# Filtered read pass of a four-layer GNN kernel: who builds the second half of the gather's one-hot columns

## The chip, the cores and the metric

One core of one Trainium2 chip. The metric is the device time of one execution of the whole program in microseconds, and the kernel before is given by the median of three executions.

## What is computed

The program runs four graph layers over 12,500 nodes and 400,000 edges (edges sorted by `dst`), with a residual and a layer norm after each:

```python
x = layernorm(x + L0(x, W, edge_weight, src, dst))          # weighted sum over edges, relu
x = layernorm(x + L1(x, src, dst, edge_attr_64, ...))       # filtered messages, below
x = layernorm(x + L2(x, edge_index, W1, b1, W2, b2))        # sum over edges, then an MLP
x = layernorm(x + L3(x, edge_index, weight, bias))          # degree-normalised sum

def L1(x, i, j, rbf, ...):                                  # i = src, j = dst
    Wxh  = x @ Wl.T + bl
    f_ij = silu(rbf @ Wf1.T + bf1) @ Wf2.T + bf2
    agg  = segment_sum(f_ij * Wxh[j], i, num_segments=12500)
    ...
```

The change touches layer L1 alone: the gather `Wxh[j]`, the product with the filter rows `f_ij` and the sum into row `i`.

## The kernel before, in words

Edges were sorted by an earlier stage (`fused`) into cells of up to 128 edges: the node rows of `dst` are cut into NW = 49 windows of 256 nodes, those of `src` into NS = 98 tiles of 128 nodes. `read_pass(1, filtered=True)` (L1326) does layer L1. It walks over GW = 14 groups of CG = 7 source tiles, and in each group over the 49 windows. One window of one group is a step: 686 steps, each over seven cells of 128 edges. Seven steps are a round (RUN = 7, seven rounds to a group). Of the seven rounds the first six are a hardware loop, with addresses and semaphore targets made from registers; the last is written out, its table offset a constant.

A step j does the following.

- **first** (VectorE, L1401 to L1409): `row` holds, on all 128 partitions, the position (1 to 256) of each of the 896 edges in its window. Two tensor_scalar instructions at L1407 compare it with partition + 1 (m = 0) and partition + 129 (m = 1, `iota2`), giving the two halves of `hot`, [128, 2, 7, 128] in bf16. Position 0 marks an empty place.
- **gather** (TensorE, L1487 to L1500): 42 matmuls (seven cells, two halves, three bf16 parts of the table) of 64 columns each gather the table's rows into PSUM. It waits for `x_hot` of its step and for `x_whole` two steps back.
- **message** (VectorE, L1418 to L1438) in three pieces: `whole` = gathered rows times filter rows (L1427), `rest` = whole minus its bf16 head (L1433), and the third part (L1437), which signals `x_msg`.
- **second** (VectorE, L1411, by way of `selection` at L552): the one-hot columns for the sum.
- **scatter** (TensorE, L1510 to L1519): seven matmuls of 193 columns into four PSUM banks. It waits for `x_sel` and `x_msg`.
- **taken** (ScalarE, L1563 to L1569): once in a group, four copies of the sums out of PSUM. `collect` (VectorE, L1440) adds the parts. After `taken`, TensorE clears the banks (L1523).

The order on each queue is written out by hand. VectorE in step j: whole(j), first(j + 2), rest(j), second(j + 1), third part(j). TensorE: gather(j + 1), scatter(j), gather(j + 2), scatter(j + 1), and so on; so gather(j + 1) is behind scatter(j - 1), which waits for third part(j - 1). `hot`, `sel` and `msg` have three buffers each, used in the order 0, 1, 0, 1, 0, 1, 2. SyncE reloads `row`, `pairs` and `f` in spans of two steps, the row after `x_hot` of the span, the pairs after `x_sel`, the filter rows after `x_whole` (L1374). ScalarE has nothing but `taken` in this pass.

`reach` (L1306) is a wait for a semaphore against a value made from the step's number, and `settle` (L132, recorded at L135) is an instruction that carries such waits.

Of the kernel before, what the change touches and what calls it, by code (L numbers as in the profile page):

```python
# [8 lines left out]
ACT = mybir.ActivationFunctionType  # L9
# [29 lines left out]
CG = 7  # L39
# [19 lines left out]
def build(nc, a, out):  # L59
    ctx = ExitStack()  # L60
    with ctx:
        def sb(name, shape, dt=F32):
            return ctx.enter_context(nc.sbuf_tensor(name, shape, dt))
# [4 lines left out]
        def counter(name):  # L68
            return Counter(ctx.enter_context(nc.semaphore(name)))
# [21 lines left out]
        identb = sb("identb", [P, P], BF16)  # L91
        iota2 = sb("iota2", [P, 2])
        iotab = sb("iotab", [P, WIN], BF16)
        iotas = sb("iotas", [P, NS], BF16)
        zerob = sb("zerob", [P, 2 * (PARTS * D + 1)], BF16)
        negb = sb("negb", [P, P], BF16)
# [49 lines left out]
        with nc.Block() as block:  # L146
            @block.sync
            def _(sp):
                for dst, src in loads:
                    sp.dma_start(dst, src).then_inc(s_load.sem, 16)  # L150
                sp.wait_ge(s_zero.sem, len(weights))
                for dst, src in blocks:
                    sp.dma_start(dst, src).then_inc(s_diag.sem, 16)
                sp.wait_ge(s_zero.sem, len(weights) + 2 * PARTS)
                for m in range(PARTS):
                    sp.dma_start(bias_b[m:m + 1, :, :], bias_p[:, m, :, :]).then_inc(s_diag.sem, 16)
                sp.wait_ge(s_load.sem, 16 * len(loads))
                sp.wait_ge(s_diag.sem, 16 * (len(blocks) + PARTS))

            @block.scalar  # L160
            def _(act):
                act.wait_ge(s_const.sem, 11)
                for w in range(NW):
                    act.dma_start(rows_d[:, w * NS * RW:(w + 1) * NS * RW].rearrange("p (k e) -> p k e", k=4),
                                  zeros[:, :].unsqueeze(1).to_broadcast([P, 4, QUARTER])).then_inc(s_clear.sem, 16)

            @block.gpsimd
            def _(pool):
                pool.memset(ident[:, :], 0.0).then_inc(s_const.sem, 1)
                pool.memset(upper[:, :], 1.0).then_inc(s_const.sem, 1)  # L170
                pool.memset(zeros[:, :], 0.0).then_inc(s_const.sem, 1)
                pool.memset(ones[:, :], 1.0).then_inc(s_const.sem, 1)
                pool.memset(onesb[:, :], 1.0).then_inc(s_const.sem, 1)
                pool.iota(iota2[:, :], pattern=[[P, 2]], base=1, channel_multiplier=1,
                          allow_small_or_imprecise_dtypes=True).then_inc(s_const.sem, 1)
                pool.iota(iotab[:, :], pattern=[[1, WIN]], base=1, channel_multiplier=0,
                          allow_small_or_imprecise_dtypes=True).then_inc(s_const.sem, 1)
                pool.iota(trash[:, :], pattern=[[0, 1]], base=ROWS, channel_multiplier=1,
                          allow_small_or_imprecise_dtypes=True).then_inc(s_const.sem, 1)
                pool.memset(strides[:, :], 1.0).then_inc(s_const.sem, 1)  # L180
                pool.memset(zerob[:, :], 0.0).then_inc(s_const.sem, 1)
                pool.iota(iotas[:, :], pattern=[[1, NS]], base=0, channel_multiplier=0,
                          allow_small_or_imprecise_dtypes=True).then_inc(s_const.sem, 1)
                pool.wait_ge(s_const.sem, 11)
                pool.memset(strides[0:1, :], float(NT)).then_inc(s_const.sem, 1)
                pool.affine_select(out=ident[:, :], in_=ident[:, :], compare_op=ALU.not_equal, fill=1.0,
                                   base=0, pattern=[[-1, P]], channel_multiplier=1).then_inc(s_const.sem, 1)

                pool.affine_select(out=upper[:, :], in_=upper[:, :], compare_op=ALU.is_ge, fill=0.0,
                                   base=0, pattern=[[1, P]], channel_multiplier=-1).then_inc(s_const.sem, 1)  # L190
                pool.wait_ge(s_const.sem, 14)
                pool.tensor_scalar(negb[:, :], ident[:, :], -1.0, None, ALU.mult).then_inc(s_const.sem, 1)
                pool.tensor_scalar(trib[:, :], ident[:, :], 1023.0, None, ALU.mult).then_inc(s_const.sem, 1)
                pool.wait_ge(s_const.sem, 16)
                pool.tensor_tensor(trib[:, :], trib[:, :], upper[:, :], ALU.add).then_inc(s_const.sem, 1)
                pool.memset(acc[:, :, :], 0.0).then_inc(s_const.sem, 1)
                pool.wait_ge(s_const.sem, 18)

            @block.vector
            def _(dve):  # L200
                for w, _name in weights:
                    dve.memset(w[:, :], 0.0).then_inc(s_zero.sem, 1)
                dve.wait_ge(s_load.sem, 16 * len(loads))
                for m in range(PARTS):
                    n = len(weights) + 2 * m
                    rest, piece = bias_r[:, m, :, :], bias_p[:, m, :, :]
                    dve.tensor_copy(piece, rest).then_inc(s_zero.sem, 1)
                    dve.wait_ge(s_zero.sem, n + 1)
                    dve.tensor_tensor(bias_r[:, m + 1, :, :], rest, piece, ALU.subtract).then_inc(s_zero.sem, 1)
                    dve.wait_ge(s_zero.sem, n + 2)  # L210
# [345 lines left out]
        def half_of_pairs(w, h):  # L556

            return dstpair_d[:, bass.ds(w * (NS * 2) + h * HALF * 2, 2 * HALF)].rearrange("p (c two) -> p c two", two=2)

        def fused():  # L560

            fctx = ExitStack()
            with fctx:
# [2 lines left out]

                raw_in = counter("raw_in")
                p_ea = [counter(f"p_ea_in_{h}") for h in range(2)]
                p_land = [counter(f"p_landed_{c}") for c in range(BC)]
                p_int, p_col, p_meta = (counter(f"p_{x}") for x in ("integers", "columns", "meta_copied"))  # L570
                p_f1, p_h, p_f2, p_rows = (counter(f"p_{x}") for x in ("f1_done", "silu_done", "f2_done", "rows_done"))
                p_o, p_t, p_q, p_nc, p_r, p_v, p_slot, p_idx = (
# [86 lines left out]
                with nc.Block() as block:  # L659
# [370 lines left out]
                    def _(act):  # L1030
# [54 lines left out]
                        act.sem_inc(e_out.sem, 64)  # L1085
                        act.sem_inc(e_by_group.sem, 16)
                        run_beats(act, beat)

        x_in, x_stored, x_dve = (counter(x) for x in ("x_in", "x_stored", "x_dve"))

# [203 lines left out]
            x_acc.base += CREDIT + NW  # L1294

        x_out = counter("x_sums_out")
        RUN = 7
        RUNS = NW // RUN
        BUFFER = (0, 1, 0, 1, 0, 1, 2)
# [26 lines left out]
        def read_pass(n, filtered=False):  # L1326
# [5 lines left out]
            with ectx:  # L1332
# [6 lines left out]
                sel = [sbe(f"sel{b}", [P, CG, P], BF16) for b in range(3)]  # L1339
                msg = [sbe(f"msg{b}", [P, CG, V], F32 if filtered else BF16) for b in range(3)]  # L1340
                kept = sbe("kept", [P, CG, V])
                got = [psb[b][:, 0:CG * D] for b in range(3)] if filtered else psb[0:BANKS]
                sums = psb[3:7] if filtered else psb[4:8]

# [8 lines left out]
                with nc.Block() as block:  # L1353
                    @block.sync
                    def _(sp):
# [18 lines left out]
                        def reload(t, g, w):  # L1374
                            for h in range(len(SPANS)):
                                reach(sp, x_hot, t, SPANS[h][1])
                                settle(sp)
                                load_row(g, w, h)
                                reach(sp, x_sel, t, SPANS[h][1])
                                settle(sp)  # L1380
# [19 lines left out]
                    def _(dve):  # L1400
                        def first(t, i, j):  # L1401
# [1 line left out]
                            run_landed(dve, x_row[h], i + j // RUN)  # L1403
                            reach(dve, x_got, t, j + 1 - AHEAD_HOT, MB)
                            settle(dve)
                            for m in range(2):
                                o = dve.tensor_scalar(hot[BUFFER[j % RUN]][:, m, :, :].rearrange("p c e -> p (c e)"),  # L1407
                                                      row[h][:, at, :], iota2[:, m:m + 1], None, ALU.is_equal)
                            o.then_inc(x_hot.sem, 1)  # L1409
# [70 lines left out]
                    def _(pe):  # L1480
# [6 lines left out]
                        def gather(t, j, e):  # L1487
                            b = BUFFER[j % RUN]
                            reach(pe, x_hot, t, j + 1)
                            if filtered:  # L1490
                                reach(pe, x_whole, t, j - 1)
                                settle(pe)
                                for c in range(CG):
# [59 lines left out]
                    def _(act):  # L1553
                        def copied_run(t):
                            for j in range(RUN):
                                reach(act, x_sum, t, j - 1)
                                for k in range(BANKS):
# [2 lines left out]
                                    act.activation(msg[BUFFER[j]][:, 2 * k:2 * k + cells_of(k), :].rearrange("p c e -> p (c e)"),  # L1560
                                                   got[k][:, 0:cells_of(k) * VW], ACT.Copy).then_inc(x_msg.sem, 1)

                        def taken(g):  # L1563
                            act.wait_ge(x_sum.sem, g * NW + x_sum.at(CREDIT + NW))
                            act.wait_ge(x_acc.sem, g * TAKEN + x_acc.at(CREDIT))
# [3 lines left out]
                                               sums[b][:, 0:cells_of(b) * V], ACT.Copy).then_inc(x_out.sem, 1)  # L1569
                        with under(act, 0):  # L1570
                            if filtered:
                                with loop(act, 0, GW) as g:
                                    taken(g)
                            else:
                                act.sem_inc(x_msg.sem, CREDIT)
                                with loop(act, 0, RUNS - 1) as r:
# [7 lines left out]
                                taken(GW - 1)  # L1584
            for c_ in x_row + x_pair + (x_f if filtered else []):
                c_.base += 16 * GW * RUNS
            for c_ in (x_hot, x_sel, x_sum) + ((x_whole, x_rest) if filtered else ()):
                c_.base += CREDIT + GW * NW
            for c_ in (x_got, x_msg):
                c_.base += CREDIT + GW * MB * NW  # L1590
# [8 lines left out]
        sem_sidx = [counter(f"sidx_in_{h}") for h in range(2)]  # L1599
        sem_ew = [counter(f"ew_in_{h}") for h in range(2)]  # L1600
        sem_ea = [counter(f"ea_in_{h}") for h in range(2)]
        sem_gath = [counter(f"gathered_{j}") for j in range(GROUP)]
        sem_tab = [counter(f"added_{k}") for k in range(TABLES)]
        sem_hl = [counter(f"hl_in_{h}") for h in range(2)]
        s_bc = counter("bcast_done")
# [382 lines left out]
```

## Time and profile before

| | us |
|---|---|
| median of 3 executions | 10044.14 |
| lowest and highest | 10036.44, 10044.95 |
| the profiled execution, its own time | 10034.89 |
| its span, first to last instruction | 10033.2 |
| busy in it: TensorE, VectorE, ScalarE, GpSimdE | 7987.4, 7207.5, 4080.3, 3286.7 |
| the filtered pass, about | 4917 to 7014 of the span |

The profiled execution is 9.3 us below the median; 1.7 us of its time lie outside its span. In the rows, PE is TensorE's matmuls, PEld its weight loads, DVE is VectorE, ACT is ScalarE, SP is SyncE; a "q" behind the name means the engine's sequencer. "idle before" is time that the engine stood still before an instruction, and the name behind "<-" is what ended that.

### The profile page before, as it was taken

How to read it: one execution, taken by the hardware profiler on the slowest of the kernel's cores; microseconds unless marked ns; L12 is line 12 of the kernel's file. 1: busy time of each engine (PE TensorE's matmuls, PEld its weight loads, DVE VectorE, ACT ScalarE, POOL GpSimd, SP SyncE). 2: the span in 40 equal slices, each digit the busy share in tenths (PEclk: the TensorE clock that was granted, in tenths of full speed). 3: DMA queues.
4: the chain of work that ended last, by engine and by line, in shares of the span. 5: the costliest groups of instructions: out<-in, count | busy, mean ns of one | idle time of the engine just before them, and what ended most of it. 6: DMA issues, size and time to landing. Idle time of an engine off the chain costs nothing. (4 is left out here: it accounts for less than half of the span.)

```text
span 10033.2 us, 322009 instructions
## 1 busy us (share of the span) xinstructions
PE 7987.4 (80%) x101781; PEld 6666.3 (66%) x101781; DVE 7207.5 (72%) x15153; ACT 4080.3 (41%) x13577; POOL 3286.7 (33%) x3158
## 2 busy tenths in 40 slices
PE   0368888888888888886577777777499999799997
PEld 0246666666666666665566666666377777699997
DVE  0246666666666667666799999999777777677777
ACT  0124444444444444444200000000477777588886
POOL 0177777777777777773000000000100000000000
PEclk9979999999999999999899999999799999899998
DMA  9734444444444444444366566655133333166664
GB/s 404 302 103 126 134 129 131 129 129 135 135 125 135 129 130 123 135 135 126 82 153 158 156 155 157 157 154 141 61 115 111 111 112 116 48 129 128 129 129 102
DMA packets 885197, 1378.29 MB, mean 137 GB/s; under 512 B 382886, under 2 KB 734310, under 8 KB 872374
## 3 DMA queue, kind: packets, MB, share of 16 engines
q1 hardware_dynamic: 759174, 1100.25, 41.2%
q10 hardware_dynamic: 25872, 167.19, 4.1%
q0 software_dynamic: 100000, 109.00, 3.5%
q8 instruction: 75, 1.23, 0.1%
q14 instruction: 76, 0.62, 0.0%
HBM read 1086.88 MB, written 289.10 MB: 137 GB/s over the span
## 5 line engine op out<-in xcount | busy, mean ns | idle before, releaser
L770 POOL DMA_INDIRECT edge_rows<-f_rows,f_index x3125 | 3242.0, 1037 | 968.1 <-issue 908.3
L552 DVE TENSOR_TENSOR x_sel<-iotab,x_pairs 128x896 bf16<-128x896 bf16 (+1 forms) x2058 | 1596.2, 776 | 369.9 <-PE ps L1261 345.6
L1038 ACT ACTIVATE f_msg<-ps,f_yew 128x64 f32<-128x64 f32 x4802 | 1058.6, 325 | 1465.9 <-PE ps L951 1426.0
L1516 PE MATMUL ps<-x_msg,x_sel 128*128 128x193 bf16 (+1 forms) x9604 | 1059.6, 250 | 479.8 <-issue 475.0
L1407 DVE TENSOR_SCALAR x_hot<-x_row,iota 128x896 bf16<-128x896 bf16 x2744 | 1112.6, 448 | 306.9 <-PE ps L1506 294.8
L1158 ACT ACTIVATE x_msg<-ps 128x384 bf16<-128x384 f32 (+1 forms) x2744 | 1014.3, 456 | 427.0 <-PE ps L1247 427.0
L1516 PEld LDWEIGHTS ps<-x_msg,x_sel 128*128 128x128 bf16 x9604 | 809.4, 98 | 542.9 <-issue 538.0
L1496 PE MATMUL ps<-tab,x_hot 128*128 (+1 forms) x28812 | 1108.0, 194 | 32.3 <-issue 27.5
L1496 PEld LDWEIGHTS ps<-tab,x_hot 128*128 128x128 bf16 x28812 | 1050.0, 99 | 84.1 <-issue 55.1
L1560 ACT ACTIVATE x_msg<-ps 128x384 bf16<-128x384 f32 (+1 forms) x2744 | 1015.9, 456 | 193.6 <-PE ps L1506 191.8
L966 PE MATMUL ps<-f_msg,f_ysel 128*128 128x192 bf16 x9604 | 993.2, 256 | 113.8 <-issue 113.7
L966 PEld LDWEIGHTS ps<-f_msg,f_ysel 128*128 128x128 bf16 x9604 | 849.1, 100 | 138.4 <-issue 123.9
L1506 PE MATMUL ps<-tab,x_hot 128*128 (+1 forms) x9604 | 914.4, 247 | 5.6 <-DVE x_hot L1407 4.8
L1261 PE MATMUL ps<-x_msg,x_sel 128*128 128x192 bf16 x9604 | 905.1, 246 | 6.7 <-issue 4.4
L1568 ACT ACTIVATE x_kept<-ps 128x386 f32<-128x386 f32 (+1 forms) x112 | 41.5, 456 | 2111.9 <-PE ps L1516 2111.9
L401 POOL TENSOR_TENSOR y_n<-y_n,gamma 128x1280 f32<-128x1280 f32 x5 | 17.9, 3587 | 2451.3 <-DVE y_n L348 2451.3
L1506 PEld LDWEIGHTS ps<-tab,x_hot 128*128 128x128 bf16 x9604 | 802.4, 98 | 22.4 <-issue 11.9
L1261 PEld LDWEIGHTS ps<-x_msg,x_sel 128*128 128x128 bf16 x9604 | 772.1, 97 | 49.9 <-issue 14.3
L826 DVE TENSOR_REDUCE f_best<-ps 128x5 int32<-128x490 f32 x625 | 417.9, 669 | 515.4 <-PE ps L993 508.6
L552 DVE TENSOR_TENSOR f_ysel<-iotab,f_ypair 128x1792 bf16<-128x1792 bf16 x686 | 743.8, 1084 | 19.4 <-PE ps L966 13.6
L1247 PE MATMUL ps<-tab,x_hot 128*128 128x192 bf16 x4802 | 624.7, 245 | 138.5 <-DVE x_hot L1199 137.4
L816 DVE TENSOR_SCALAR f_total<-ps 128x98 f32<-128x98 f32 x625 | 161.8, 259 | 765.8 <-PE ps L981 747.2
(165 smaller groups left out, 11553.6 us busy)
## 6 DMA issues: line engine op xcount, KB each, us to landing
x_row<-edge_row_dst SPq DMA_DIRECT2D x588, 448.0 KB, 4.9
edge_rows<-zeros ACTq DMA_DIRECT2D x49, 3332.0 KB, 36.9
f_piece<-edge_rows SPq DMA_DIRECT2D x343, 476.0 KB
f_yrow<-edge_row_src SPq DMA_DIRECT2D x686, 224.0 KB
x_row<-edge_row_src SPq DMA_DIRECT2D x98, 1568.0 KB, 6.3
x_f<-edge_rows SPq DMA_DIRECT2D x294, 476.0 KB, 3.7
edge_rows<-f_rows,f_index POOLq DMA_INDIRECT x3125, 2.2
x_row<-edge_row_dst SPq DMA_DIRECT2D x196, 224.0 KB, 3.5
```

What stands on the lines that cost most here:

```text
L552: return dve.tensor_tensor(sel[:, :, :].rearrange("p c (e two) -> p c e two", two=2), iotab[:, 0:columns].rearrange("p (e two) -> p e two" ...
L770: pool.indirect_dma_start(out=rowbuf, out_offset=bass.IndirectOffsetOnAxis(ap=index[:, j:j + 1], axis=0), in_=rows[:, j, :], in_offset=Non ...
L966: i = pe.matmul(sums[m], ysel[g % 2][:, c, m * P:(m + 1) * P], parts, start=False, stop=g == GW - 1 and c == CG - 1 and m == 1)
L1038: i = act.activation(msg[g % 2][:, c, 0, :], got[g % 2][:, c * D:(c + 1) * D], ACT.Copy, scale=yew[h][:, lo + c:lo + c + 1])
L1158: act.activation(msg[g % 2][:, 2 * b:2 * b + m, :, :].rearrange("p c k d -> p (c k d)"), got[b][:, 0:m * PARTS * D], ACT.Copy).then_inc(x_ ...
L1247: i = pe.matmul(got[b][:, at:at + PARTS * D], hot[g % 2][:, c, :], tab3[:, g * CG + c, :, :].rearrange("p k d -> p (k d)"), start=True, st ...
L1261: i = pe.matmul(sums[m], sel[g % 2][:, c, m * P:(m + 1) * P], msg[g % 2][:, c, :, :].rearrange("p k d -> p (k d)"), start=False, stop=g == ...
L1407: o = dve.tensor_scalar(hot[BUFFER[j % RUN]][:, m, :, :].rearrange("p c e -> p (c e)"), row[h][:, at, :], iota2[:, m:m + 1], None, ALU.is_ ...
L1496: o = pe.matmul(got[b][:, c * D:(c + 1) * D], hot[b][:, m, c, :], piece(e, m * VW + k * D, D), start=m == 0 and k == 0, stop=m == 1 and k ...
L1506: o = pe.matmul(got[k][:, c % 2 * VW:(c % 2 + 1) * VW], hot[b][:, m, c, :], piece(e, m * VW, VW), start=m == 0, stop=m == 1)
L1516: o = pe.matmul(sums[c // 2][:, c % 2 * V:(c % 2 + 1) * V], sel[b][:, c, :], upper_half(msg[b][:, c, :]) if filtered else msg[b][:, c, :], ...
L1560: act.activation(msg[BUFFER[j]][:, 2 * k:2 * k + cells_of(k), :].rearrange("p c e -> p (c e)"), got[k][:, 0:cells_of(k) * VW], ACT.Copy).t ...
```

## The change

A third constant `upper_index` holds -(129 + partition). ScalarE now builds half m = 1 of `hot`: `away` = |row - (129 + partition)|, then max(0, 1 - away), which is 1 where they are equal and 0 at every other integer. VectorE builds half m = 0 alone. TensorE's gather and SyncE's reload of the row wait for ScalarE's `x_high` as well. `taken` stands in ScalarE's queue behind the high halves of the next group's first two steps. The gather semaphores of a far pass are shared with `fused` (to free semaphores for the new counters). The unfiltered read pass is unchanged.

```diff
+        upper_index = sb("upper_index", [P, 1])
...
+                pool.iota(upper_index[:, :], pattern=[[0, 1]], base=-(P + 1), channel_multiplier=-1,
+                          allow_small_or_imprecise_dtypes=True).then_inc(s_const.sem, 1)
...
+                away = sbe("away", [P, CG * P], BF16) if filtered else None
...
                             for h in range(len(SPANS)):
                                 reach(sp, x_hot, t, SPANS[h][1])
                                 settle(sp)
+                                if filtered:
+                                    reach(sp, x_high, t, SPANS[h][1])
+                                    settle(sp)
                                 load_row(g, w, h)
...
-                            for m in range(2):
+                            for m in range(1 if filtered else 2):
                                 o = dve.tensor_scalar(hot[BUFFER[j % RUN]][:, m, :, :].rearrange("p c e -> p (c e)"),
                                                       row[h][:, at, :], iota2[:, m:m + 1], None, ALU.is_equal)
...
                             reach(pe, x_hot, t, j + 1)
                             if filtered:
+                                reach(pe, x_high, t, j + 1)
                                 reach(pe, x_whole, t, j - 1)
                                 settle(pe)
...
+                        def high(t, i, j):
+                            h, at = place(j)
+                            run_landed(act, x_row[h], i + j // RUN)
+                            reach(act, x_got, t, j + 1 - AHEAD_HOT)
+                            reach(act, x_high, t, j)
+                            settle(act)
+                            act.activation(away[:, :], row[h][:, at, :], ACT.Abs, bias=upper_index[:, 0:1]).then_inc(x_away.sem, 1)
+                            reach(act, x_away, t, j + 1)
+                            settle(act)
+                            act.activation(hot[BUFFER[j % RUN]][:, 1, :, :].rearrange("p c e -> p (c e)"), away[:, :], ACT.Relu,
+                                           bias=ones[:, 0:1], scale=-1.0).then_inc(x_high.sem, 1)
+
+                        def high_run(t, i, last=False):
+                            for j in range(AHEAD_HOT, RUN if last else RUN + AHEAD_HOT):
+                                high(t, i, j)
...
                             if filtered:
-                                with loop(act, 0, GW) as g:
+                                for s in (x_away, x_high):
+                                    act.sem_inc(s.sem, CREDIT)
+                                for j in range(AHEAD_HOT):
+                                    high(0, 0, j)
+                                with loop(act, 0, RUNS - 1) as r:
+                                    high_run(step_of(act, 0, r), r)
+                                with loop(act, 0, GW - 1) as g:
+                                    high_run(step_of(act, g, RUNS - 1), run_of(act, g, RUNS - 1))
                                     taken(g)
+                                    with loop(act, 0, RUNS - 1) as r:
+                                        high_run(step_of(act, g + 1, r), run_of(act, g + 1, r))
+                                high_run(step_of(act, GW - 1, RUNS - 1), GW * RUNS - 1, True)
+                                taken(GW - 1)
```

## Rows read from the trace of the kernel before

**Rows 1.** The page: busy time of each engine over the whole span.
```profile
PE 7987.4 (80%) x101781; PEld 6666.3 (66%) x101781; DVE 7207.5 (72%) x15153; ACT 4080.3 (41%) x13577; POOL 3286.7 (33%) x3158
```

**Rows 2.** Windows view of the pass: us, PE, PEld, DVE, ACT, POOL busy, clock, DMA.
```profile
4917.00:7014.00 2097.00, 1567.15 (x33652) 1447.70 (x33652) 2021.96 (x4139) 19.30 (x52) 0.00 (x0) 0.98 0.60 156
```

**Rows 3.** Groups of instructions by line and form, in the pass.
```profile
L1407 DVE TENSOR_SCALAR x_hot<-x_row,iota 128x896 bf16<-128x896 bf16 x1372 | 553.0, 445 | 4.9 <-DMA x_row<-edge_row_dst 4.9
```

**Rows 4.** Timeline of an ordinary looped step: start us, us, engine, line.
```profile
5231.74 0.68 DVE L1437 TENSOR_TENSOR x_msg<-x_msg 128x448 bf16<-128x448 f32 x1
...
5232.31 0.61 DVE L1427 TENSOR_TENSOR x_msg<-ps,x_f 128x448 f32<-128x448 f32 x1
...
5232.52 0.78 PE L1516 MATMUL ps<-x_msg,x_sel 128*128 128x193 bf16 x7 [0.68 <-issue]
5232.83 0.81 DVE L1407 TENSOR_SCALAR x_hot<-x_row,iota 128x896 bf16<-128x896 bf16 x2
...
5233.14 1.58 PE L1496 MATMUL ps<-tab,x_hot 128*128 x42
...
5233.56 0.62 DVE L1433 TENSOR_TENSOR x_msg<-x_msg 128x448 f32<-128x448 f32 x1
...
5234.63 0.68 DVE L1437 TENSOR_TENSOR x_msg<-x_msg 128x448 bf16<-128x448 f32 x1
5235.19 0.62 DVE L1427 TENSOR_TENSOR x_msg<-ps,x_f 128x448 f32<-128x448 f32 x1
...
5235.41 0.79 PE L1516 MATMUL ps<-x_msg,x_sel 128*128 128x193 bf16 x7 [0.68 <-issue]
```

**Rows 5.** Timeline where a looped round ends and the next begins, PE and DVE.
```profile
5244.07 0.79 PE L1516 MATMUL ps<-x_msg,x_sel 128*128 128x193 bf16 x7 [0.70 <-issue]
5245.13 1.85 PE L1496 MATMUL ps<-tab,x_hot 128*128 x42 [0.28 <-issue]
...
5247.16 0.62 DVE L1427 TENSOR_TENSOR x_msg<-ps,x_f 128x448 f32<-128x448 f32 x1 [0.18 <-PE ps L1496]
```

**Rows 6.** Timeline of PE in the written-out round of a group.
```profile
5215.07 1.39 PE L1496 MATMUL ps<-tab,x_hot 128*128 128x64 bf16 x42
```

**Rows 7.** Instructions of PE's sequencer, and one of DVE's, by line (ns min/median/max).
```profile
L1496 PEldq ALU_OP  x3444: 32/32/32, 4919.3 to 6990.8; - x192
...
L1308 DVEq EVENT_SEMAPHORE  x7: 21/21/21, 6992.5 to 7013.1; - x7
...
L135 PEldq EVENT_SEMAPHORE  x12179: 51/51/17129, 430.3 to 9964.1; - x200
...
L1535 PEldq COMPARE_BRANCH  x168: 80/223/247, 4941.7 to 9953.5; - x168
```

**Rows 8.** DVE's waits in the pass: us in total, times, longest.
```profile
DVE x_msg L1427 <- PE ps L1496: 69.8, 96, 3.8
```

**Rows 9.** Timeline at a change of group.
```profile
5221.20 1.48 ACT L1568 ACTIVATE x_kept<-ps 128x386 f32<-128x386 f32 x4 [148.13 <-PE ps L1516]
...
5226.51 0.62 DVE L1427 TENSOR_TENSOR x_msg<-ps,x_f 128x448 f32<-128x448 f32 x1 [3.51 <-PE ps L1496]
```

**Rows 10.** ACT's groups by form in the whole span, with one table load.
```profile
L360 ACT ACTIVATE xT_n<-ps 128x512 f32<-128x512 f32 x40 | 23.8, 596 | 65.3 <-PE ps L357 65.3
L464 ACT ACTIVATE tab<-y_n 128x512 bf16<-128x512 f32 x30 | 18.8, 626 | 13.2 <-DVE y_n L461 13.0
...
L423 ACT ACTIVATE hT_n<-ps,b1d 128x512 f32<-128x512 f32 x10 | 6.9, 686 | 16.2 <-PE ps L419 16.2
...
L474 ACT ACTIVATE tab<-x_rows 128x1280 bf16<-128x1280 f32 x5 | 6.3, 1263 | 3.2 <-DVE x_rows L348 2.9
...
L346 ACT ACT_TABLE_LOAD x1 | 1.3, 1283 | 0.0
```

**Rows 11.** DVE's groups in the unfiltered read pass, with ACT at work beside it.
```profile
L1407 DVE TENSOR_SCALAR x_hot<-x_row,iota 128x896 bf16<-128x896 bf16 x1372 | 559.6, 450 | 302.0 <-PE ps L1506 294.8 <-DMA x_row<-edge_row_dst 6.5 <-issue 0.7
```

**Rows 12.** DMA issues in the pass: KB each, median us to landing.
```profile
x_row<-edge_row_dst SPq DMA_DIRECT2D x291, 448.0 KB, 5.0
```

More of the change, by code:

```diff
@@ L161, in _ @@
             def _(act):
-                act.wait_ge(s_const.sem, 11)
+                act.wait_ge(s_const.sem, 12)
                 for w in range(NW):
@@ L183, in _ @@
                           allow_small_or_imprecise_dtypes=True).then_inc(s_const.sem, 1)
-                pool.wait_ge(s_const.sem, 11)
+                pool.iota(upper_index[:, :], pattern=[[0, 1]], base=-(P + 1), channel_multiplier=-1,
+                          allow_small_or_imprecise_dtypes=True).then_inc(s_const.sem, 1)
+                pool.wait_ge(s_const.sem, 12)
                 pool.memset(strides[0:1, :], float(NT)).then_inc(s_const.sem, 1)
@@ L190, in _ @@
                                    base=0, pattern=[[1, P]], channel_multiplier=-1).then_inc(s_const.sem, 1)
-                pool.wait_ge(s_const.sem, 14)
+                pool.wait_ge(s_const.sem, 15)
                 pool.tensor_scalar(negb[:, :], ident[:, :], -1.0, None, ALU.mult).then_inc(s_const.sem, 1)
                 pool.tensor_scalar(trib[:, :], ident[:, :], 1023.0, None, ALU.mult).then_inc(s_const.sem, 1)
-                pool.wait_ge(s_const.sem, 16)
+                pool.wait_ge(s_const.sem, 17)
                 pool.tensor_tensor(trib[:, :], trib[:, :], upper[:, :], ALU.add).then_inc(s_const.sem, 1)
                 pool.memset(acc[:, :, :], 0.0).then_inc(s_const.sem, 1)
-                pool.wait_ge(s_const.sem, 18)
+                pool.wait_ge(s_const.sem, 19)
             @block.vector
@@ L558, in half_of_pairs @@
             return dstpair_d[:, bass.ds(w * (NS * 2) + h * HALF * 2, 2 * HALF)].rearrange("p (c two) -> p c two", two=2)
+        sem_gath = [counter(f"gathered_{j}") for j in range(GROUP)]
         def fused():
@@ L568, in fused @@
                 p_ea = [counter(f"p_ea_in_{h}") for h in range(2)]
-                p_land = [counter(f"p_landed_{c}") for c in range(BC)]
+                p_land = sem_gath[0:BC]
                 p_int, p_col, p_meta = (counter(f"p_{x}") for x in ("integers", "columns", "meta_copied"))
@@ L1087, in _ @@
                         run_beats(act, beat)
+                for c in range(BC):
+                    p_land[c].base += 16 * CHUNK * (NW if c < chunks(NW - 1) else NW - 1)
         x_in, x_stored, x_dve = (counter(x) for x in ("x_in", "x_stored", "x_dve"))
@@ L1296, in build @@
         x_out = counter("x_sums_out")
+        x_away, x_high = (counter(f"x_{x}_done") for x in ("away", "high"))
         RUN = 7
@@ L1586, in read_pass @@
                 c_.base += 16 * GW * RUNS
-            for c_ in (x_hot, x_sel, x_sum) + ((x_whole, x_rest) if filtered else ()):
+            for c_ in (x_hot, x_sel, x_sum) + ((x_whole, x_rest, x_away, x_high) if filtered else ()):
                 c_.base += CREDIT + GW * NW
@@ L1601, in build @@
         sem_ea = [counter(f"ea_in_{h}") for h in range(2)]
-        sem_gath = [counter(f"gathered_{j}") for j in range(GROUP)]
         sem_tab = [counter(f"added_{k}") for k in range(TABLES)]
```

## The prediction

> **What bounds the kernel now.** I began with the page: no engine is busy throughout the program [rows 1], so the shares say nothing and the pass has to be read by itself. The windows view of the pass shows VectorE busy for 2022 of 2097 us and ScalarE for 19 [rows 2]. The pass is 686 steps, so 3.06 us a step, 2.95 of them VectorE's. The waits view says VectorE stood still before `whole` for 69.8 us in 96 waits, the longest 3.8 us [rows 8]. VectorE is the bound, then, and ScalarE is free.
>
> The timeline must also say how far behind the next bound is. In an ordinary looped step `whole` starts at 5232.31 and again at 5235.19: 2.88 us, no idle time [rows 4]. TensorE's turn in it is a chain: the third part(j - 1) ends at 5231.74 + 0.68 = 5232.42, scatter(j - 1) starts at 5232.52, gather(j + 1) ends at 5233.14 + 1.58 = 5234.72. Where VectorE does wait for a gather, at the end of a round, it starts 0.18 after the gather's end (5245.13 + 1.85 = 5246.98 to 5247.16 [rows 5]). So `whole` could have started at 5234.90 and started at 5235.19: **the slack is 0.29 us a step**. That is the number on which this forecast rests.
>
> **What is removed.** One of the two instructions at L1407 in each step. A single one takes 0.445 us [rows 3], two from start to end take 0.81 [rows 4], so the second costs 0.81 - 0.445 = 0.365 of the queue's time; I use 0.36. VectorE's own step becomes 2.88 - 0.36 = 2.52. Were VectorE alone to decide, the 686 steps less the 98 where it waits for TensorE anyway (one a round: 96 waits are counted) would save 588 x 0.36 = 212 us. But 0.36 is more than the slack of 0.29, so in looped rounds at most 0.29 is to be had: TensorE's chain takes over.
>
> **What is added on ScalarE.** Two ACTIVATEs over 896 columns. From SBUF, 512 columns take 626 ns and 1280 take 1263 [rows 10], so 0.83 ns a column, and 896 take 626 + 384 x 0.83 = 945. A bias from a column adds 686 - 596 = 90 ns [rows 10]: 1.035 us each, 2.07 for both. The second waits for the first; a hand-over between engines takes 0.10 (5232.42 to 5232.52 [rows 4]), and with one before each the cycle is about 2.3 us, under 2.52 and under any step here. It is not a bound unless an estimate is off by a tenth or more. Lateness: high(j) may start when gather(j - 2) is done and is needed when gather(j) starts, two steps less one gather later: 2 x 2.6 - 1.6 = 3.6 us. It takes 2.3, so 1.3 are left. Were that cover gone, each microsecond of lateness would be one of the step's. For VectorE beside a working ScalarE the nearest row is the unfiltered pass, 450 ns against 445 [rows 3, 11]: nothing.
>
> `taken` stands behind two high halves. The second of these starts with the last gather of the group, one step ahead of the last scatter, and is over by then; `taken`'s four copies last 1.48 [rows 9] and TensorE goes through them as before. The next high half, about 2.3 us after `taken`, is needed after a clearing, a gather and a scatter, about 4 us: covered. The stall of 3.5 us at a change of group [rows 9] stays.
>
> **What is added on TensorE.** One more wait ahead of each gather. In the written-out round a gather takes 1.39 us [rows 6], in the looped ones 1.58 [rows 4], with six register operations of 32 ns in its midst (3444 in 574 gathers [rows 7]). So in looped rounds the gather already waits for its sequencer, and an instruction put ahead of it there is paid in full. `settle` so far carries two waits here; where three waits come with no register operation between them, the trace has one on an instruction of its own (seven at L1308 on VectorE, in the last round [rows 7]). Such a one is 51 ns on TensorE [rows 7] plus what lies between two sequencer instructions. Bounds: zero or a shade less, if the wait rides on another instruction; the register operations cost (1.58 - 1.39)/6 = 0.03 each, partly hidden; at the end of a round, scatter start to gather end is 5246.98 - 5244.07 = 2.91 [rows 5] against 5234.72 - 5232.52 = 2.20 [rows 4], 0.71 for about five more sequencer instructions, among them a branch of 0.22 [rows 7]: 0.10 to 0.14 each. I take **0.12**, the sequencer being the limit in both places, and keep 0 and 0.15 (and 0.2 if the wait comes with a register operation) for the range.
>
> **The rest.** SyncE waits for `x_high` before a row's reload. That queue issues a row only behind the previous span's filter load, which waits for `whole`, two steps later than the hot columns; a row lands 5.0 us after its issue [rows 12] and is used some five steps, 13 us, later. Nothing, unless DMA at 0.60 of its time [rows 2] slows much at 0.64. The start of the pass: high(0) and high(1) take 2.3 each where two compares took 0.8; about 2 us once. The iota and the shared semaphores: under 0.3 us, bounded by nothing but the start.
>
> **The sum.** In each of 14 groups: 35 ordinary looped steps gain 0.29 - 0.12 = 0.17, 5.95 us; 7 steps that wait for TensorE already lose 0.12, 0.84 us; 7 of the written-out round, where the gather is 0.19 shorter and the new wait hidden, gain the full 0.36, 2.5 us. That is 7.6 a group, 107 in all, less 2: **105 us**. Against the profiled execution's own 10034.9 this is 9930; it stood 9.3 below the median, so for a median I say 10044 - 105 = 9939.
>
> **A rule that speaks against it.** In the Trainium skill, ScalarE: Activation LUTs, section "Rules for kernel authors" says that relu-like work belongs on VectorE, which is several times as fast per element in bf16. The rows agree on the price: 2.07 us on ScalarE in place of 0.36 on VectorE. By the rule taken as it stands the move would lose, which is the second rival; the sum goes by who is idle.
>
> **The rivals.**
> (1) The wait is free. Then the looped steps gain 0.29: 14 x (35 x 0.29 + 7 x 0.36) = 177, giving 9867; if the chain is also shorter than I read, up to 212, giving 9832. For it: the waits already ride on other instructions wherever one is near. Against: rows 7. Chance 0.17.
> (2) The gain is eaten. ScalarE's pair takes 2.9 us, or the extra wait on TensorE costs 0.3: the step stays near 2.88, 10044 +- 20. For it: no row shows Abs, nor a bf16 input from SBUF. Against: it needs each ACTIVATE at 1.3 us, a quarter above the rows. Chance 0.07.
> (3) Slower: ScalarE becomes the bound because Abs and Relu need different tables. Each load is 1.283 us [rows 10], two a step make the pair 2.3 + 2.57 = 4.9 against 3.06 now: 686 x 1.8 = 1250 more, 11290. It decides from a pair of 3.06 us on, one load a step being enough. Against: the Relu with a bias at L423 [rows 10] stands among copies and square roots, and no table load is recorded at its line. Chance, with milder forms of a late ScalarE (10060 to 10300), 0.08.
> The same page, section "Table sets: the hidden batching unit", says that relu and abs are in every set; by that (3) can't happen, and the trace agrees for Relu, while no row shows Abs.
> (4) The change does not do what it says: VectorE's L1407 would still be there twice. The diff leaves no room for it.
>
> **How the numbers follow.** The forecast has 0.68: 9939, and its own bounds are 9898 (a wait of 0.05) to 9986 (one of 0.2), by the same sum. The range adds the free wait and most of the way to the eaten gain: 9850 to 10005. About 0.2% (20 us) is what a measurement here can tell from no change. Faster: 0.68 + 0.17 = 0.85; same 0.07; slower 0.08.
>
> **What the profile after would show.** L1407 x686 in the pass and VectorE busy about 1770 us; two ACTIVATEs of about 1.03 us, 686 each; an ordinary looped step of about 2.71 us, with VectorE now waiting at L1427 for TensorE in most of them (some 500 waits, not 96); an extra semaphore instruction of 51 ns before the looped gathers, and scatter start to gather end at 2.32 instead of 2.20; the written-out round at 2.52 a step. I am wrong if VectorE still never waits (then the slack was misread), if TensorE waits for `x_high`, or if table loads appear between the ACTIVATEs.

## The result, and the profile after

The kernel after takes 9876.79 us in the median of four executions (9872.93 to 9880.05), the kernel before 10040.9 beside it: ratio 0.9837, 95% interval 0.9823 to 0.9852. That is 164 us less; the prediction said 105 less, for a median of 9939 in a range of 9850 to 10005. The sign and the range held, and so did the forecast that VectorE stops being the bound and the chain through TensorE takes over. The gain was half as large again as forecast, which is clear of the noise and needs a cause.

All of it is in the filtered pass. First and last start of `whole` (line view of the kernel after, then windows view over just that stretch, columns as in [rows 2]):

```profile
L1439 DVE TENSOR_TENSOR x_msg<-ps,x_f x686: 598/625/639, 4926.6 to 6844.6; 128x448 f32<-128x448 f32 x172
```
```profile
4926.60:6844.60 1918.00, 1597.96 (x33610) 1474.58 (x33610) 1802.91 (x3450) 1443.42 (x1420) 0.00 (x0) 0.98 0.69 169
```

The same line of the kernel before:

```profile
L1427 DVE TENSOR_TENSOR x_msg<-ps,x_f x686: 597/612/640, 4920.0 to 7013.9; 128x448 f32<-128x448 f32 x172
```

2093.9 us became 1918.0, 176 less. VectorE lost 686 instructions, and ScalarE went from 19 us of work [rows 2] to 1443. The span fell by 162 (10033.2 to 9871.0); 6.6 of the other 14 us are a later start of the pass, and 7.1 are the stages behind it (3019.3 to 3026.4 from the last `whole` to the end). More on those at the end.

The groups that answer to [rows 3] and to what the prediction said of ScalarE, with all of ScalarE's table loads in the whole span (groups by line and form):

```profile
L1582 ACT ACTIVATE x_away<-x_row,upper_index 128x896 bf16<-128x896 bf16 x686 | 715.2, 1043 | 371.7 <-PE ps L1509 347.7 <-ACT x_hot L1585 16.8 <-DMA x_row<-edge_row_dst 7.2
L1585 ACT ACTIVATE x_hot<-x_away,ones 128x896 bf16<-128x896 bf16 x686 | 714.9, 1042 | 82.6 <-ACT x_away L1582 2.9
L363 ACT ACT_TABLE_LOAD x1 | 1.3, 1283 | 382.6 <-PEq L147 382.6
L272 ACT ACT_TABLE_LOAD x1 | 1.3, 1283 | 10.2 <-PE ps L269 10.2
L349 ACT ACT_TABLE_LOAD x1 | 1.3, 1283 | 0.0
L396 ACT ACT_TABLE_LOAD x1 | 1.3, 1283 | 7.1 <-PEq L1940 7.1
```

1042 and 1043 ns against the 1035 worked out. ScalarE waits for TensorE before most pairs, for 348 us in all: it has time to spare. Four loads in the program and none in the pass, so Abs and Relu share a table with what was there, as the Trainium skill says (ScalarE: Activation LUTs, "Table sets: the hidden batching unit").

TensorE waited for ScalarE's half at the start of the pass alone, once and for 6.2 us. The kernel before waited there for VectorE's halves for 4.7, so the start costs about 1.5 us, where the forecast had 2.

The wait on TensorE did get an instruction of its own, 686 of them at the line of `reach` (sequencer instructions by line, ns min/median/max):

```profile
L1316 PEldq EVENT_SEMAPHORE  x686: 51/51/51, 4916.5 to 6841.6; - x172
```

And the timeline of ordinary looped steps, which answers to [rows 4] (start us, us, engine, line):

```profile
5149.74 0.70 DVE L1449 TENSOR_TENSOR x_msg<-x_msg 128x448 bf16<-128x448 f32 x1
...
5150.52 0.62 DVE L1439 TENSOR_TENSOR x_msg<-ps,x_f 128x448 f32<-128x448 f32 x1
5150.54 0.79 PE L1529 MATMUL ps<-x_msg,x_sel 128*128 128x193 bf16 x7 [0.20 <-issue]
...
5151.17 1.71 PE L1509 MATMUL ps<-tab,x_hot 128*128 x42
...
5152.49 0.68 DVE L1449 TENSOR_TENSOR x_msg<-x_msg 128x448 bf16<-128x448 f32 x1
...
5153.06 0.62 DVE L1439 TENSOR_TENSOR x_msg<-ps,x_f 128x448 f32<-128x448 f32 x1
...
5153.28 0.79 PE L1529 MATMUL ps<-x_msg,x_sel 128*128 128x193 bf16 x7 [0.40 <-issue]
...
5153.90 1.69 PE L1509 MATMUL ps<-tab,x_hot 128*128 x42
...
5155.77 0.63 DVE L1439 TENSOR_TENSOR x_msg<-ps,x_f 128x448 f32<-128x448 f32 x1
```

Scatter start to gather end is 5152.88 - 5150.54 = 2.34 and then 5155.59 - 5153.28 = 2.31, where it was 2.20: the new instruction costs 0.11 to 0.14, as taken. But `whole` starts at 5150.52, 5153.06 and 5155.77, steps of 2.54 and 2.71 in turn. The forecast had 2.71 for each. **Every second step is nearly as short as VectorE allows (2.52). The forecast held every step up by TensorE's chain, and only every second one is.**

### The profile page after: what moved, and what is told of

Same layout as the page of the kernel before. It is cut to its first block and busy times, and to the rows that moved or that the text cites. A ratio compares the mean times of both kernels' runs of the same rounds, so it can differ in the third digit from the quotient of the medians.

```text
span 9871.0 us, 327048 instructions
## 1 busy us (share of the span) xinstructions
PE 8013.5 (81%) x101781; PEld 6690.5 (68%) x101781; DVE 6989.5 (71%) x14467; ACT 5509.6 (56%) x14949; POOL 3298.4 (33%) x3159
## 5 line engine op out<-in xcount | busy, mean ns | idle before, releaser
L1509 PE MATMUL ps<-tab,x_hot 128*128 (+1 forms) x28812 | 1154.3, 194 | 39.7 <-DVE x_hot L1419 26.9
L1509 PEld LDWEIGHTS ps<-tab,x_hot 128*128 128x128 bf16 x28812 | 1085.4, 99 | 102.7 <-issue 63.6
L1419 DVE TENSOR_SCALAR x_hot<-x_row,iota 128x896 bf16<-128x896 bf16 x2058 | 865.5, 449 | 316.6 <-PE ps L1519 300.5
L1519 PE MATMUL ps<-tab,x_hot 128*128 (+1 forms) x9604 | 915.9, 247 | 8.5 <-DVE x_hot L1419 5.8
L1582 ACT ACTIVATE x_away<-x_row,upper_index 128x896 bf16<-128x896 bf16 x686 | 715.2, 1043 | 371.7 <-PE ps L1509 347.7
L1519 PEld LDWEIGHTS ps<-tab,x_hot 128*128 128x128 bf16 x9604 | 803.5, 98 | 25.8 <-issue 14.9
L1585 ACT ACTIVATE x_hot<-x_away,ones 128x896 bf16<-128x896 bf16 x686 | 714.9, 1042 | 82.6 <-ACT x_away L1582 2.9
```

What stands on the lines that cost most here:

```text
L1509: o = pe.matmul(got[b][:, c * D:(c + 1) * D], hot[b][:, m, c, :], piece(e, m * VW + k * D, D), start=m == 0 and k == 0, stop=m == 1 and k ...
L1519: o = pe.matmul(got[k][:, c % 2 * VW:(c % 2 + 1) * VW], hot[b][:, m, c, :], piece(e, m * VW, VW), start=m == 0, stop=m == 1)
L1582: act.activation(away[:, :], row[h][:, at, :], ACT.Abs, bias=upper_index[:, 0:1]).then_inc(x_away.sem, 1)
```

## The theory, and its rivals

Follow one `whole` to the one that it holds up. whole(j - 1) starts at 5150.52; the third part of that step ends at 5153.17; scatter(j - 1) starts at 5153.28; gather(j + 1) ends at 5155.59; whole(j + 1) starts at 5155.77, 0.18 later. The loop over VectorE and TensorE closes over **two** steps, 2.65 + 0.11 + 2.31 + 0.18 = 5.25 us. The 2.65 in it is VectorE's own work, one step of 2.54 and the 0.11 by which `whole` may start before the third part ahead of it has ended. Theory A: in looped steps the pass runs at half that loop, 2.62 us, and each saving or cost in the gather's chain counts half per step. Theory B is the prediction's: the loop closes over one step and each 0.12 counts in full. Theory C: the chain is no bound at all, and VectorE or ScalarE sets the pace. The runs change the chain's length without touching VectorE.

## The experiments

A pass is given as the stretch from the first to the last start of `whole`, from each profile's row for that line. Times of different groups were taken on different chips (the kernel before: 10019 us in the first group, 10047 in the second), so kernels are compared within a group or by their ratio to the kernel before.

Two steps in one timeline can mislead, so here is where the time of each pass lies: the times from one start of `whole` to the next, added up over the whole trace, in us. "Behind the branch" is the second step of each looped round, whose gather is the first in the body of TensorE's loop over rounds; 13 of the 84 have the change of group in them. "Ordinary" are the other looped steps, without the first of a group, and "last round" is the written-out one.

| | steps | before | e7_before_wait | after | e2_more_waits | e9_two_waits_again | e5_written_out |
|---|---|---|---|---|---|---|---|
| ordinary | 490 | 1423.5 | 1422.8 | 1291.2 | 1329.1 | 1264.1 | 1246.5 |
| behind the branch | 84 | 312.9 | 322.8 | 302.8 | 302.5 | 287.0 | 238.0 |
| last round | 98 | 317.3 | 317.9 | 280.4 | 282.3 | 279.5 | 286.6 |
| first of a group | 13 | 40.2 | 40.6 | 43.6 | 44.1 | 43.6 | 44.0 |

Within the looped rounds of the kernel after the steps go in turn all through the pass: counted from 0, steps 2, 4 and 6 of a round take 2.54, 2.55 and 2.56 us on average and steps 3 and 5 take 2.72 and 2.71.

### One wait fewer (e1_two_waits, e9_two_waits_again)

```diff
                                 reach(pe, x_high, t, j + 1)
-                                reach(pe, x_whole, t, j - 1)
                                 settle(pe)
```

> The kernel after, less TensorE's wait for x_whole before each gather. That wait is implied already: scatter(j - 2) stands ahead of gather(j) in TensorE's queue and waits for the third part(j - 2), which follows whole(j - 2). Two waits ride on one instruction, so the lone semaphore instruction should go. Theory A (the loop over TensorE and VectorE closes over two steps, so what a gather's chain saves is halved in each step): scatter start to gather end falls from 2.34 to 2.21 us in looped steps, the mean looped step by 0.06, the pass by about 30 us: about 9846. Theory B (the loop closes over one step, as the prediction had it): the pass falls by about 55 us: about 9822. Theory C (VectorE or ScalarE is the bound after the change and the extra instruction costs nothing): no change, 9877.

Measured: 9806.5 us, ratio 0.9785 (0.9768 to 0.9801). The lone instructions are gone and looped steps look so (timeline, TensorE and then VectorE at `whole`):

```profile
5152.86 0.79 PE L1528 MATMUL ps<-x_msg,x_sel 128*128 128x193 bf16 x7 [0.93 <-issue]
5153.48 1.56 PE L1508 MATMUL ps<-tab,x_hot 128*128 x42
```
```profile
5152.65 0.61 DVE L1439 TENSOR_TENSOR x_msg<-ps,x_f 128x448 f32<-128x448 f32 x1
5155.22 0.62 DVE L1439 TENSOR_TENSOR x_msg<-ps,x_f 128x448 f32<-128x448 f32 x1
5157.77 0.62 DVE L1439 TENSOR_TENSOR x_msg<-ps,x_f 128x448 f32<-128x448 f32 x1
```

The line view of `whole` in the same profile:

```profile
L1439 DVE TENSOR_TENSOR x_msg<-ps,x_f x686: 597/624/633, 4936.2 to 6811.5; 128x448 f32<-128x448 f32 x172
```

Scatter start to gather end is 5155.04 - 5152.86 = 2.18, two steps take 5157.77 - 5152.65 = 5.12 (theory A: 5.25 - 0.13). The pass is 1875.3, 43 less. Theory C is out. Against the kernel after the ratio is 0.0052 lower, about 52 us, which is near B's 55, and the pass lay between A's 30 and B's 55. So the same kernel was run again beside the kernel after on one chip:

> The kernel of e1_two_waits again, beside the kernel after on one chip. In its first profile the pass was 43 us shorter than in the kernel after (theory A had said 30 from the ordinary steps alone, theory B 55). Theory A with the loop ends counted: 40 to 45 us under the kernel after. Theory B: 55 or more.

Measured: 9840.69 (ratio 0.9796, 0.9783 to 0.9810) beside 9878.85 for the kernel after: 38 less, the passes 1874.2 and 1915.2, 41 less. The pair of steps settles it: -0.13 for two steps and not for each. So does the table: against the kernel after, the 490 ordinary steps lose 27 us, 0.055 each, where theory A has 0.06 and theory B 0.11. Another 16 us, 0.19 each, come from the 84 steps behind the branch, where `whole` waits for the gather in every round and a saving counts in full. Neither theory had priced these before the first run.

### One wait more (e2_more_waits)

```diff
                                 reach(pe, x_whole, t, j - 1)
                                 settle(pe)
+                                reach(pe, x_high, t, j + 1)
+                                settle(pe)
```

> The kernel after, with one more wait for x_high before each gather, on an instruction of its own; it never has to wait. Theory A (two-step loop): scatter start to gather end grows by 0.11 to 2.45 us in looped steps, the mean looped step by 0.055, the pass by about 28 us: about 9905. Theory B (one-step loop): the pass grows by about 50 us: about 9928. Theory C (TensorE's chain is not the bound): no change, 9877.

Measured: 9878.42, ratio 0.9861 (0.9845 to 0.9878), where the kernel after has 0.9837: 0.24% or 24 us slower. The pass is 1958.0, 40 longer than 1918.0, so it lies between A's 28 and B's 50. Timeline:

```profile
5153.09 0.61 DVE L1439 TENSOR_TENSOR x_msg<-ps,x_f 128x448 f32<-128x448 f32 x1
5155.96 0.62 DVE L1439 TENSOR_TENSOR x_msg<-ps,x_f 128x448 f32<-128x448 f32 x1 [0.22 <-PE ps L1511]
5158.50 0.61 DVE L1439 TENSOR_TENSOR x_msg<-ps,x_f 128x448 f32<-128x448 f32 x1
5161.38 0.62 DVE L1439 TENSOR_TENSOR x_msg<-ps,x_f 128x448 f32<-128x448 f32 x1 [0.23 <-PE ps L1511]
```

Steps of 2.87, 2.54 and 2.88: 5.42 for two, some 0.15 over the kernel after. One of the two steps pays and the other does not, as theory A says. It holds throughout: 38 of the 40 us are in the ordinary steps, where steps 3 and 5 of a round become 0.12 and 0.15 longer and steps 2, 4 and 6 at most 0.02. From scatter start to gather end the instruction costs 0.13 to 0.20 (medians by place in the round) and not the 0.11 expected, which is a good part of why 28 became 40.

### The high half left out (e4_no_high)

```diff
                                 reach(pe, x_hot, t, j + 1)
-                                reach(pe, x_high, t, j + 1)
                                 settle(pe)
...
-                                for j in range(AHEAD_HOT):
-                                    high(0, 0, j)
...
+                                with loop(act, 0, GW) as g:
                                     taken(g)
```

> The kernel of e1_two_waits, with the high half left out altogether: ScalarE builds nothing, nobody waits for x_high, and the second half of the three one-hot buffers is zeroed once at the start. It leaves out what the second half of every window contributes to the gather. If ScalarE's part is free: the same as e1_two_waits within 5 us. If ScalarE's 1.04 us instructions or their lateness cost anything (contention, a late x_high in some steps, late row reloads): faster than e1_two_waits by that.

Measured: 9810.67, ratio 0.9793 (0.9777 to 0.9809), against 0.9785 for e1_two_waits in the same group; pass 1880.5 against 1875.3. No faster without ScalarE. The whole of the moved work, its 1372 ACTIVATEs, its waits and SyncE's wait before a row, costs nothing that these runs can tell. What the change costs is TensorE's one instruction and about 1.5 us at the start.

### A third ACTIVATE (e6_third_activate)

```diff
                             act.activation(away[:, :], row[h][:, at, :], ACT.Abs, bias=upper_index[:, 0:1]).then_inc(x_away.sem, 1)
+                            act.activation(spare[:, :], row[h][:, at, :], ACT.Abs, bias=upper_index[:, 0:1])
```

> The kernel after, with a third ACTIVATE of 896 columns into a spare buffer between the two of each step. ScalarE's cycle, 2.41 us where it is not held up in the profile after, grows by 0.95 to 1.04 to about 3.4 us and must become the bound: about 3.4 x 686 = 2330 us for the pass in place of 1929, 10280 in all, TensorE waiting for x_hot of ScalarE in every step. If there is still cover (the ahead-building absorbs it), it would stay near 9877; that would contradict the reading that ScalarE decides from a cycle of about 2.6 us on.

Measured: 10083.13 in one execution, 64 over the kernel before on that chip. ScalarE's timeline:

```profile
5159.50 1.04 ACT L1583 ACTIVATE x_away<-x_row,upper_index 128x896 bf16<-128x896 bf16 x1 [0.20 <-ACT x_hot L1587]
5160.44 1.03 ACT L1584 ACTIVATE x_spare<-x_row,upper_index 128x896 bf16<-128x896 bf16 x1
5161.38 1.02 ACT L1587 ACTIVATE x_hot<-x_away,ones 128x896 bf16<-128x896 bf16 x1
5162.60 1.04 ACT L1583 ACTIVATE x_away<-x_row,upper_index 128x896 bf16<-128x896 bf16 x1 [0.20 <-ACT x_hot L1587]
```

ScalarE is the bound, with a cycle of 3.10 and not the 3.4 expected: the third instruction starts 0.94 after the first and fills the time in which Relu had waited for Abs (1.16 from start to start before), so it adds 0.7. The pass is 2148.4, 54.5 over the kernel before. 686 x 3.10 would be 2127, but the nearness is in part chance: in the last round of a group the first steps take 2.5 to 2.9 us, and the step over a change of group takes 5.8. So rival (3) of the prediction, a ScalarE too slow, had its place about right: it decides from 3.06 on, and 3.10 loses. The real cycle is 2.41 where nothing holds it up. No run has a cycle between these two.

### The kernel after once more (e8_after_again)

The same kernel, nothing edited; it is the base for the second group.

> The kernel after, unchanged, so that the others of this group can be read against it on one chip. Between 9850 and 9880 us, 1.6% under the kernel before, the pass (first to last x_sel) 1921 us in its profile. How far the other stages move in it shows how much of 162 us is the pass: the pass alone was 174 us shorter.

Measured: 9878.85, ratio 0.9835 (0.9821 to 0.9848), pass 1915.2. The gain repeats.

### The wait in the kernel before (e7_before_wait)

```diff
                                 reach(pe, x_whole, t, j - 1)
                                 settle(pe)
+                                reach(pe, x_hot, t, j + 1)
+                                settle(pe)
```

> The kernel before, with one more wait before each gather on an instruction of its own, which never has to wait. Theory A: over two steps TensorE's chain has 0.29 us to spare there, so the 0.12 us of the instruction is hidden in ordinary steps and paid only where VectorE waits for TensorE, about seven times in a group: 98 x 0.12 to 0.2, 12 to 20 us slower. If the instruction is paid in every looped step: 588 x 0.12 = 70 us slower.

Measured: 10053.84 beside 10046.58, ratio 1.0008 (0.9999 to 1.0017). These 7 us are inside the noise, and the 70 us of an instruction paid in every looped step are excluded. The trace says more (TensorE, and VectorE at `whole`):

```profile
5240.15 0.61 DVE L1427 TENSOR_TENSOR x_msg<-ps,x_f 128x448 f32<-128x448 f32 x1
5240.36 0.79 PE L1518 MATMUL ps<-x_msg,x_sel 128*128 128x193 bf16 x7 [1.45 <-issue]
5240.99 1.73 PE L1498 MATMUL ps<-tab,x_hot 128*128 x42
5243.03 0.61 DVE L1427 TENSOR_TENSOR x_msg<-ps,x_f 128x448 f32<-128x448 f32 x1
5245.92 0.62 DVE L1427 TENSOR_TENSOR x_msg<-ps,x_f 128x448 f32<-128x448 f32 x1
```

Scatter start to gather end is now 5242.72 - 5240.36 = 2.36 and not 2.20, yet the steps are 2.88 and 2.89 as before. The pass is 2104.0 against 2093.9, and 9.9 of these 10 us are in the 84 steps behind the branch, 0.12 each; the 490 ordinary steps pay nothing. That is the pattern of theory A (12 to 20 us). Had the slack been 0.29 in each step, the ordinary steps would have hidden this instruction as well; so it is e1, e2 and the kernel after that tell one step from two, and this run says that there was cover to hide it in. The instruction has a price in ordinary steps only since the change took the cover away.

### TensorE's rounds written out (e5_written_out)

On top of e1_two_waits:

```diff
                         def rounds(g):
+                            if filtered:
+                                for r in range(RUNS - 1):
+                                    run(step_of(pe, g, r), r * RUN * WROW, (r + 1) * RUN * WROW)
+                                return
                             with loop(pe, 0, RUNS - 1) as r:
```

> The kernel of e1_two_waits with all seven rounds of TensorE's queue written out in the filtered pass, so that the table's addresses are constants: no register operations in the gather, no branch at the end of a round. Theory A: scatter start to gather end is 2.01 us in every step, the pair of steps over TensorE is 2.64 + 2.01 + 0.27 = 4.92, shorter than two VectorE steps of 2.53, so VectorE is the bound everywhere but at a change of group: 686 x 2.53 + 13 x 1.9 + 13 x 3 = 1800 us for the pass, some 75 under e1_two_waits and 120 under the kernel after. Rival: a straight stream of code, six times as long, can't be fetched as fast as it is used, and waits named issue take the place of the branch; then the gain is less, or a loss.

Measured: 9777.52, ratio 0.9737 (0.9724 to 0.9750), 101 under the kernel after and 63 under e9_two_waits_again in the same group. Timeline of TensorE, of VectorE at `whole`, and the line view of `whole`:

```profile
5150.13 0.78 PE L1528 MATMUL ps<-x_msg,x_sel 128*128 128x193 bf16 x7 [0.63 <-issue]
5150.75 1.38 PE L1508 MATMUL ps<-tab,x_hot 128*128 128x64 bf16 x42
```
```profile
5149.91 0.61 DVE L1439 TENSOR_TENSOR x_msg<-ps,x_f 128x448 f32<-128x448 f32 x1
5152.44 0.62 DVE L1439 TENSOR_TENSOR x_msg<-ps,x_f 128x448 f32<-128x448 f32 x1
5154.96 0.61 DVE L1439 TENSOR_TENSOR x_msg<-ps,x_f 128x448 f32<-128x448 f32 x1
```
```profile
L1439 DVE TENSOR_TENSOR x_msg<-ps,x_f x686: 597/612/645, 4929.0 to 6744.0; 128x448 f32<-128x448 f32 x172
```

With 2.00 us from scatter start to gather end, the steps are 2.53 and 2.52: VectorE's own time, with no alternation left. The pass is 1815.0 (expected 1800). The edit takes away the register operations and the branch together, and the table tells their shares: of the 59 us that this pass is shorter than that of e9_two_waits_again, 49 come from the steps behind the branch and 18 from the ordinary ones, while the last rounds lose 7. Longer code did not starve TensorE in ordinary steps. The loss in the last rounds, where TensorE's queue jumps back to the head of its loop over groups, may be the rival at work in small; no run tests it. This version beats both kernels.

## Why the prediction was right, and where it missed

**What bounds the kernel**: right. VectorE gave the step, and the 0.29 us of slack was where it was read, though it is there once for two steps (below).

**What is removed**: right. 0.36 us is the difference between 2.88 and the 2.52 that VectorE needs where nothing holds it up (e5_written_out). VectorE was busy for 1803 us and not 1770: where `whole` is held up, it no longer starts before the third part has ended, and time that the two shared is now counted for each.

**ScalarE**: right to 8 ns on each instruction; the cover of 1.3 us held, and e4_no_high shows the move itself to be free. The rule that such work belongs on VectorE (the Trainium skill, ScalarE: Activation LUTs, "Rules for kernel authors") names up to about three times per element in bf16. The rows agree: 1042 ns on ScalarE for 896 columns against 445 on VectorE [rows 3] for one instruction, and 2.08 us against 0.36 for the whole job. e6_third_activate shows how near this price is to deciding. With ScalarE idle it did not decide. (The prediction calls the loss by this rule "the second rival"; of its numbered rivals it is (3), since (2) is no change.)

**The added wait on TensorE**: right, with one exception. It has its own instruction of 51 ns and costs 0.11 to 0.14 in the chain. In one step of a looped round, the one behind the wait at the branch, it costs nothing, as rival (1) had it for all (the kernel after):

```profile
5225.92 0.79 PE L1529 MATMUL ps<-x_msg,x_sel 128*128 128x193 bf16 x7
...
5226.55 1.62 PE L1509 MATMUL ps<-tab,x_hot 128*128 x42
```

Here scatter start to gather end is 2.25, and the median of the 84 such places is 2.21. That the total of 9877 came near rival (1)'s 9867 is chance: its cause, a wait that costs nothing, is not what happened.

**The sum**: here is the step that failed, "35 ordinary looped steps gain 0.29 - 0.12 = 0.17". Both numbers were right and their use was wrong. The 0.29 is spare in a loop over two steps, and the prediction held it against one step's saving of 0.36, as if every step were held up by TensorE. The loop also has a VectorE step in it, from whole(j - 1) to the end of third part(j - 1), which the change shortens by the same 0.36. Worked anew from rows of before alone: 3.00 (5232.31 to 5235.31) + 0.10 + 2.20 + 0.18 = 5.48 for two steps, where two steps took 5.77 and so had the 0.29 to spare; less 0.36, plus 0.12, is 5.24 (measured 5.25). A step gains 2.88 - 2.62 = 0.26 and not 0.17; 0.09 x 490 is 44 us, so 107 should have been 151. The table of the passes has 132 us less in the 490 ordinary steps, 0.27 each.

Most of the other 25 us of the pass's 176 lie at round ends and changes of group. The prediction charged 98 such steps with 12 us in all; the steps behind the branch and the first of a group together became 7 us shorter, which makes 19. Ordinary steps gained 5 more than the 0.26 gives, and the last rounds 37 where the prediction had 35. At a change of group (the kernel after, DVE at `whole`):

```profile
5201.25 0.63 DVE L1439 TENSOR_TENSOR x_msg<-ps,x_f 128x448 f32<-128x448 f32 x1 [0.51 <-issue]
5207.23 0.63 DVE L1439 TENSOR_TENSOR x_msg<-ps,x_f 128x448 f32<-128x448 f32 x1 [3.32 <-PE ps L1509]
```

5.98 us, where before it went from 5220.01 to 5226.51, 6.50: the chain through TensorE starts from a third part that now ends 0.36 earlier in its step. That is the same oversight in another place, as far as one can argue from these rows; no run tests the pieces of this remainder.

**What the profile would show**: "some 500 waits" at `whole` was wrong as a sign. The waits view of the kernel after has fewer than before [rows 8]:

```profile
DVE x_msg L1439 <- PE ps L1509: 85.8, 90, 3.6
```

`whole` can start 0.11 before the third part ahead of it has ended, so a hold-up of 0.2 leaves at most 0.1 of idle time between them, and the view doesn't list it. With the longer chain of e2_more_waits the idle time is 0.22, and the same view lists 322 waits. In the kernel after the hold-up shows in start-to-start times alone.

## What to carry to other kernels

When a queue gets shorter, follow the chain through the other engine from one instruction to the one that it releases, and count the steps that it spans: slack of a loop that closes over two steps is there once for both of them, and the shortened engine's own part of the chain gets shorter too. Count the waits on the next engine's instruction: the third one in front of a gather cost 41 us of a pass in which the change gained 176, and here one of the three was implied by a wait already made. Writing the rounds out, with constant addresses and no branch, took the rest of the queue's overhead away, and the branch was the larger part. A slow instruction on an idle engine is free as long as its cycle fits in the step: here 2.41 us cost nothing and 3.10 lost, and what lies between was not run. The rows of the kernel before put the cycle at 2.3 and the step at 2.88, which was close enough to judge the move in advance.

## What the runs showed of the hardware that was not expected

- Three ACTIVATEs of 896 columns that need not wait for the one just ahead follow each other at 0.94 us (e6_third_activate), while two of which the second waits for the first are 1.16 apart from start to start (the kernel after): 0.22 us is the price of that dependence on one engine.
- A semaphore instruction of 51 ns ahead of a gather made TensorE's chain 0.11 to 0.20 us longer in nearly every looped step, and not at all in the written-out rounds, where scatter start to gather end is 2.01 us before and after.
- Six rounds of straight code in TensorE's queue in place of one looped round (e5_written_out) brought no loss in ordinary steps: they ran at 2.00 us from scatter start to gather end, step after step.
- The stages ahead of the pass and behind it, whose work is the same in all kernels, moved from profile to profile: first `whole` between 4906.4 (e2_more_waits) and 4937.3 (e9_two_waits_again), and for the kernel after 4926.6 once and 4936.4 once. That is as large as some of the effects studied, so each was read from the pass as well as from the total. What moves them stays open.
